# Byte rows for the first expansion, and its key gathers split in two, in a graph network kernel on one Trainium2 core

## The reference

```
edge network: h = relu([x_src, x_dst] @ W1.T + b1); v = h @ W2.T + b2, once for (src, dst), once for (dst, src)
              each v gives a Householder reflection; messages to src and to dst, scaled by 1/sqrt(deg) of both ends
              x = layernorm(x + relu(x - sum of messages))
two convolutions: h = tanh(segment_sum((h @ W)[src] * norm, dst) + b)
              x = layernorm(x + h)
```

## Time and profile before

| | |
|---|---|
| median of 3 runs | 7013.33 us |
| profiled execution, its time from first to last instruction (its span) | 7361.5 us |
| VectorE busy | 6335.9 us, 86% |
| ScalarE busy | 4842.1 us, 66% |
| TensorE matmul busy | 4369.6 us, 59% |
| GpSimd busy | 2840.7 us, 39% |
| first expansion | 1404 to 2343 us |
| key stage | 2345 to 2394 us |
| edge network | 2394 to 4700 us |

### The profile page before, as it was taken

One profiled execution on the slowest core, in us unless ns is written; L12 is line 12 of the kernel. 1 busy time (PEld: TensorE's weight loads), 2 busy tenths in 40 slices (PEclk: granted clock), 3 DMA queues, 4 the chain that ended last, 5 costly groups with the idle time before them and its releaser, 6 DMA issues.

```text
span 7361.5 us, 242681 instructions
## 1 busy us (share of the span) xinstructions
PE 4369.6 (59%) x83922; PEld 3504.3 (48%) x83922; DVE 6335.9 (86%) x9628; ACT 4842.1 (66%) x13310; POOL 2840.7 (39%) x2217
## 2 busy tenths in 40 slices
PE   1442000376665888888888888766566655566554
PEld 0342000266664555555555555555456544565443
DVE  4679997344445899999999999999999999999999
ACT  1665104122222899999999999899666677566776
POOL 5222304566764222222222222278500388200686
PEclk6666555688887898999889998887765699666898
DMA  4100000488876333333333333244499644799444
GB/s 63 8 8 8 4 0 26 148 297 298 299 288 218 120 117 118 116 118 116 116 116 116 117 117 117 88 121 120 105 294 291 211 120 120 200 293 295 127 121 95
DMA packets 510685, 1043.90 MB, mean 142 GB/s; under 512 B 125636, under 2 KB 316452, under 8 KB 497540
## 3 DMA queue, kind: packets, MB, share of 16 engines
q1 hardware_dynamic: 376804, 761.05, 30.1%
q0 software_dynamic: 113920, 281.72, 15.9%
q10 hardware_dynamic: 19872, 0.11, 0.2%
HBM read 756.44 MB, written 286.18 MB: 142 GB/s over the span
## 4 chain that ended last, share of the span: by engine, by line
DVE 28%; issue 27%; PE 12%; ACT 10%; POOL 10%; DVEq 5%; ACTq 3%; another core or an unknown queue 2%; DMA 1%; SPq 0%; POOLq 0%
PE ps L1118 7%; POOL got L638 4%; POOL sw_inb L638 4%; DVE xs_ring L1864 4%; PE ps L1259 3%; DVE wide_hotb L1987 3%; DVE keys L1476 3%; DVEq L1758 3%; ACT apartb L959 2%; DVE lane_hot L1754 2%; ACT step_lo L738 2%; DVE prods L1832 2%; ACTq L1006 2%; DVE keys L1475 2%
## 5 line engine op out<-in xcount | busy, mean ns | idle before, releaser
L638 POOL DMA_INDIRECT xs_ring<-xd_rows,src_idx x488 | 595.3, 1220 | 1803.8 <-DVE xs_ring L1864 1663.8
L1987 DVE TENSOR_SCALAR wide_hotb<-sw_inb,slot_id 128x2048 bf16<-128x2048 bf16 x976 | 923.2, 1014 | 57.5 <-PE ps L1259 57.3
L1754 DVE TENSOR_TENSOR wide_hotb<-dst_key,iota_b 128x1792 bf16<-128x1792 bf16 x879 | 949.0, 1080 | 8.5 <-ACT val_out L1017 4.4
L1259 PE MATMUL ps<-wide_tabb,wide_hotb 128*128 128x48 bf16 x15616 | 640.1, 207 | 360.9 <-DVE wide_hotb L1987 232.3
L638 POOL DMA_INDIRECT got<-val_rows,dst_idx x296 | 396.7, 1340 | 1177.3 <-DMA val_rows<-val_out 1085.9
L1118 PE MATMUL ps<-row_tab,dst_hot 128*128 128x64 bf16 x15744 | 656.0, 203 | 295.7 <-issue 244.9
L1259 PEld LDWEIGHTS ps<-wide_tabb,wide_hotb 128*128 128x128 bf16 x15616 | 592.0, 112 | 409.2 <-ACT val_out L1017 315.2
L1148 PEld LDWEIGHTS ps<-wide_tab,wide_hot 128*128 128x128 bf16 x23424 | 617.8, 99 | 347.8 <-DVE wide_hot L1748 309.1
L1118 PEld LDWEIGHTS ps<-row_tab,dst_hot 128*128 128x128 bf16 x15744 | 577.1, 104 | 374.9 <-issue 340.0
L638 POOL DMA_INDIRECT src_key<-chunk_keys,src_idx x488 | 622.0, 1275 | 335.5 <-ACT xd_out L801 187.3
L1148 PE MATMUL ps<-wide_tab,wide_hot 128*128 128x32 bf16 x23424 | 642.4, 181 | 89.0 <-DVE wide_hot L1748 84.0
(11 more groups left out here) (416 smaller groups left out, 11818.9 us busy)
## 6 DMA issues: line engine op xcount, KB each, us to landing
dw_in<-dst_wide SPq DMA_DIRECT2D x96, 1312.0 KB
xd_rows<-xd_out SPq DMA_DIRECT2D x128, 984.0 KB
sw_in<-src_wide SPq DMA_DIRECT2D x244, 512.0 KB
sw_inb<-src_wide SPq DMA_DIRECT2D x244, 512.0 KB, 5.1
val_rows<-val_out SPq DMA_DIRECT2D x488, 192.0 KB, 4.1
sw_inb<-src_byte SPq DMA_DIRECT2D x244, 256.0 KB, 4.4
msg_rows<-msg_out SPq DMA_DIRECT2D x244, 200.0 KB, 2.8
dw_in<-dst_byte SPq DMA_DIRECT2D x32, 656.0 KB
```

Of the source, the lines that this page charges most:

```text
L638: return pool.indirect_dma_start(out=into, out_offset=None, in_=table, in_offset=bass.IndirectOffsetOnAxis(index, 0))
L1259: last = mm(ps_val[s * 2 + h][:, t, :], wide_hot2[s][:, half, e:e + P], wide_tab2[s][:, h, half * 3 * D:(half + 1) * 3 * D], start=half == ...
L1754: return v.tensor_tensor(to.rearrange("p t (j k) -> p t j k", k=2), rel.unsqueeze(2).to_broadcast(shape), iota_b[:, 0:w].rearrange("p (j k ...
L1987: last = v.tensor_scalar(wide_hot2[q % 2][:, half, :], sw_in2[q][:, :], slot_id[:, half:half + 1], None, ALU.is_equal)
```

## The change

All rows of the first expansion are loaded as bytes. POOL gathers only `NA` = 288 steps of keys beside it (five steps in every two rows). The key stage works on these 288 x 8 = 2304 keys, in a form with fewer operations, and only 18 tiles are transposed and stored, the byte copy from the same transposes. The other 200 steps are gathered in the first 100 turns of the edge network, two steps in each, behind the turn's two row gathers, into the part of `dst_part` that is not used yet. In pass `MID` = 30 of the edge network's loop (counted from 0, so the 31st; it stands outside the hardware loop now) they are worked on in four rounds, one ahead of each turn. After the pass ACT and PE wait until all of it is done.

```diff
+    NA = 288
+    MID = 30
+    RATE = 2
+    TURNS = 4
+    ROUND = TURNS * P // CH
+    ROUNDS = ceil_div(NST - NA, ROUND)
+    PIECE = 256 // CH
...
-        dw_in = [sb(f"dw_in{k}", [P, WID], U8 if k == 3 else BF16, of=pc) for k in range(4)]
+        dw_in = [sb(f"dw_in{k}", [P, WID], U8, of=pc) for k in range(4)]
...
-                rows = dst_byte_v if k == 3 else dst_wide_v
+                rows = dst_byte_v
...
             sp.wait_ge(wide_stored, 32)
+            sp.wait_ge(rel_ready, 2)
...
+            def store_turned(r):
+                at = tiles_of(r)
+                sp.wait_ge(turn_copied, r + 3)
+                sp.dma_start(turn_v[:, at, :], turned_b[:, 0:at.stop - at.start, :]).then_inc(wide_stored, 16)
+                sp.dma_start(turn8_v[:, at, :], turned_b8[:, 0:at.stop - at.start, :]).then_inc(wide_stored, 16)
...
-            for s in range(NST):
-                if s % 4 == 0:
-                    pool.wait_ge(unit_copied, 3 * (2 + s // 4))
+            for s in range(NA):
+                if s % 5 == 0:
+                    pool.wait_ge(unit_copied, 3 * (2 + s // 5 * 2))
...
+                for s in range(NA + RATE * g, min(NA + RATE * g + RATE, NST)):
+                    gather(raw_b[:, (s - NA) * CH:(s - NA + 1) * CH], chunk_keys, src_idx[:, s:s + 1]).then_inc(keys_got, 16)
...
+            def copy_turned(r):
+                n = tiles_of(r).stop - tiles_of(r).start
+                act.wait_ge(rel_turned, r + 2)
+                if r > 0:
+                    act.wait_ge(wide_stored, 32 + 32 * r)
+                act.activation(turned_b[:, 0:n, :], ps_turn_b[:, 0:n, :], ACT.Copy)
+                act.activation(turned_b8[:, 0:n, :], ps_turn_b[:, 0:n, :], ACT.Copy).then_inc(turn_copied, 1)
...
+            for q in range(4):
+                turn(MID, q)
+                copy_turned(q)
+            act.wait_ge(rel_ready, ROUNDS + 4)
...
+            def turn_keys(r):
+                at = tiles_of(r)
+                pe.wait_ge(rel_ready, r + 4)
+                pe.wait_ge(xt_copied, MID * 4 + r + 2)
+                for c in range(at.start, at.stop):
+                    last = nc.tensor.transpose(ps_turn_b[:, c - at.start, :], src_rel[:, c * P:(c + 1) * P], ident_b[:, :])
+                last.then_inc(rel_turned, 1)
...
             step(v.tensor_scalar(half_i[:, :], half_i[:, :], 2 * P - 1, None, ALU.bitwise_and))
-            v.tensor_copy(src_low[:, 0:n], half_i[:, :]).then_inc(rel_ready, 1)
-            dve.wait_ge(rel_ready, 2)
-            step(v.tensor_tensor(missing[:, :], src_rel[:, 0:n], src_low[:, 0:n], ALU.not_equal))
-            step(v.tensor_scalar(missing[:, :], missing[:, :], 4.0 * P, None, ALU.mult))
-            step(v.tensor_tensor(dst_rel[:, 0:n], dst_rel[:, 0:n], missing[:, :], ALU.add))
+            step(v.tensor_tensor(missing[:, :], src_rel[:, 0:n], half_i[:, :], ALU.not_equal))
+            step(v.scalar_tensor_tensor(dst_rel[:, 0:n], missing[:, :], 4.0 * P, dst_rel[:, 0:n], ALU.mult, ALU.add))
...
+            def late_keys(r):
+                if r == 0:
+                    dve.wait_ge(keys_got, 16 * NST)
+                end = min(NA + (r + 1) * ROUND, NST)
+                for a in range(NA + r * ROUND, end, PIECE):
+                    b = min(a + PIECE, end)
+                    m, at, k = (b - a) * CH, slice(a * CH, b * CH), slice((a - NA) * CH, (b - NA) * CH)
+                    whole, half, gone, low_dst = raw_b_i[:, k], half_b[:, 0:m], missing_b[:, 0:m], dst_rel_b[:, 0:m]
+                    step(v.tensor_copy(whole, raw_b[:, k]))
+                    step(v.tensor_scalar(half, whole, 8, None, ALU.arith_shift_right))
+                    step(v.tensor_tensor(src_rel[:, at].rearrange("p (s c) -> p s c", c=CH), half.rearrange("p (s c) -> p s c", c=CH),
+                                         wide_base[:, a:b].unsqueeze(2).to_broadcast([P, b - a, CH]), ALU.subtract))
+                    v.tensor_scalar(whole, whole, 2 * P - 1, None, ALU.bitwise_and)
+                    step(v.tensor_scalar(half, half, 2 * P - 1, None, ALU.bitwise_and))
+                    step(v.tensor_tensor(gone, src_rel[:, at], half, ALU.not_equal))
+                    step(v.scalar_tensor_tensor(low_dst, gone, 4.0 * P, whole, ALU.mult, ALU.add))
+                    step(v.tensor_scalar(dst_part[:, at, 1], low_dst, float(P), None, ALU.is_ge))
+                    step(v.scalar_tensor_tensor(dst_part[:, at, 0], dst_part[:, at, 1], -float(P), low_dst, ALU.mult, ALU.add))
+                dve.sem_inc(rel_ready, 1)
+
+            def late_upper(r):
+                at = slice((NA + r * ROUND) * CH, min(NA + (r + 1) * ROUND, NST) * CH)
+                dve.wait_ge(rel_turned, r + 2)
+                step(v.tensor_scalar(src_upper[:, at], src_rel[:, at], float(P), None, ALU.is_ge))
+                step(v.scalar_tensor_tensor(src_rel[:, at], src_upper[:, at], -float(P), src_rel[:, at], ALU.mult, ALU.add))
+
+            with dve.Fori(1, MID) as i:
+                four_turns(i)
+            four_turns(MID)
+            late_upper(ROUNDS - 1)
+            dve.sem_inc(rel_ready, 1)
```

More of the change, by code:

```diff
@@ L52, in gnn_kernel @@
     G = NST // 2
+    assert NA % (P // CH) == 0 and ROUNDS == 4 and RATE * (4 * MID - 4) >= NST - NA and 8 * MID + 8 <= NA - 8
     assert NST % 4 == 0
@@ L136, in gnn_kernel @@
         place = sb("place", [P, WID], of=po)
+        before = sb("before", [P, P], of=po)
+        first = sb("first", [P, P], of=po)
+        iota_f = sb("iota_f", [P, P], of=po)
         follow = sb("follow", [P, P], of=po)
@@ L682, in _ @@
             pool.wait_ge(wide_stored, 32)
+            pool.wait_ge(rel_ready, 2)
             for g in range(G):
@@ L815, in _ @@
             act.wait_ge(rel_turned, 1)
[L816 to L822, removed]
+            for to in (turned, turned_8):
+                for b in range(0, NA * CH // P, 8):
+                    end = min(b + 8, NA * CH // P)
+                    last = act.activation(to[:, b:end, :], ps_turn[:, b:end, :], ACT.Copy)
+                last.then_inc(turn_copied, 1)
             act.wait_ge(wide_stored, 32)
-            act.wait_ge(rel_ready, 4)
+            act.wait_ge(rel_ready, 3)
             def tables(i, q):
@@ L934, in _ @@
                 turn(0, q)
-            with act.Fori(1, LAST) as i:
+            def copy_turned(r):
[5 more added lines that the diff above has]
+                act.activation(turned_b8[:, 0:n, :], ps_turn_b[:, 0:n, :], ACT.Copy).then_inc(turn_copied, 1)
+            with act.Fori(1, MID) as i:
+                for q in range(4):
+                    turn(i, q)
+            for q in range(4):
+                turn(MID, q)
+                copy_turned(q)
+            act.wait_ge(rel_ready, ROUNDS + 4)
+            with act.Fori(MID + 1, LAST) as i:
                 for q in range(4):
@@ L1126, in _ @@
                     expand_row(i, k)
-            pe.wait_ge(rel_ready, 2)
-            for c in range(LW * CH // P):
+            pe.wait_ge(rel_ready, 1)
+            for c in range(NA * CH // P):
                 last = nc.tensor.transpose(ps_turn[:, c, :], src_rel[:, c * P:(c + 1) * P], ident_b[:, :])
-            last.then_inc(rel_turned, 1)
-            for c in range(LW * CH // P):
-                last = nc.tensor.transpose(ps_turn8[:, c, :], src_low[:, c * P:(c + 1) * P], ident_b[:, :])
             last.then_inc(rel_turned, 1)
@@ L1206, in _ @@
                 turn(0, q)
-            with pe.Fori(1, LAST) as i:
+            def turn_keys(r):
[5 more added lines that the diff above has]
+                last.then_inc(rel_turned, 1)
+            with pe.Fori(1, MID) as i:
+                for q in range(4):
+                    turn(i, q)
+            for q in range(4):
+                turn(MID, q)
+                turn_keys(q)
+            pe.wait_ge(turn_copied, ROUNDS + 2)
+            with pe.Fori(MID + 1, LAST) as i:
                 for q in range(4):
@@ L1889, in _, with four_turns @@
             begun = done[0]
-            with dve.Fori(1, LAST) as i:
-                done[0], base[0] = 0, i * (LINKS * 4) + (begun - LINKS * 4)
+            extra = [0]
+            def four_turns(i):
+                done[0], base[0] = 0, i * (LINKS * 4) + (begun - LINKS * 4 + extra[0])
                 for q in range(4):
+                    if isinstance(i, int):
+                        late_keys(q)
+                        if q > 0:
+                            late_upper(q - 1)
                     turn(i, q)
-                assert done[0] == LINKS * 4, done[0]
@@ L1896, in _ @@
+            extra[0] = done[0] - LINKS * 4
+            dve.sem_inc(rel_ready, 1)
+            with dve.Fori(MID + 1, LAST) as i:
+                four_turns(i)
+            base[0], done[0] = 0, begun + (LAST - 1) * LINKS * 4 + extra[0]
             for q in range(4):
```

65 lines of the change are left out of this document (39 added, 26 removed).

## The result

The changed kernel takes 6907.88 us in the median of 4 runs (6905.14 to 6910.77), the kernel before 7013.13: a ratio of 0.9841, 95% interval 0.9819 to 0.9863, 105 us faster. The forecast was 6867, 146 faster.

What follows compares the result with a forecast made beforehand. DMA was taken to pace the first expansion, DVE the edge network. Expansion -171, key stage -14 and edge network +32 gave -153 us, scaled to -146: 7013 to 6867 us, 8-in-10 range 6745 to 6998.

Steps and rivals of the forecast that it cites:

- Part 1, the row: First expansion, all rows as bytes: a row falls from 7.34 to 6.0 us, 171 us saved over 128 rows.
- rival A: First expansion: PE's gaps shrink and DVE's floor sets the row, 4.75 to 5.2 us; 6733 us in all; chance 0.12.
- loop through PE: Expansion: copy, choose, hot and PE take 5.05 + P for two rows, P being PE's time on a row; 4.9 a row.
- sign of being right: Expected if the forecast holds: expansion of 740 to 800 us, DMA under 0.8 at about 280 GB/s.
- Part 1, POOL: First expansion: 2.5 gathers a row cost POOL at most 6.05 us, with 12 rows left to cover lateness.
- 0.953: Median 7013 over profiled span 7361.5; scales the summed change from -153 to -146 us, as the trace doesn't place the 348.
- Part 2, the key stage: Key stage: DVE's chain falls from 36.3 to 21.9 us, 14.4 saved; the other chain, 19.7, stays hidden.
- Part 3, the edge network: Edge network: moved gathers hidden, DVE's late work 25 us, the stall after pass 31 7 us; +32 in all.
- Rival D: Edge network: each of 200 gathers holds one DVE operation for 1.22 us, +244; 7100 us in all; chance 0.03.
- Rival B: First expansion: PE's 245 us of issue gaps stay, a row is 7.0 us; 6994 us in all; chance 0.16.
- Rival C: First expansion: the byte hot sits on each row's path, +132 us; 7156 us in all, slower; chance 0.07.

Runs made afterwards that it cites:

- late_wait: Changed kernel with ACT's wait for the late keys one pass of the edge network later: 7214.92 us, ratio 0.9814, where the kernel before took 7348.5.
- bytes_alone: Kernel before with all 128 rows as bytes and nothing else, all 488 key gathers still beside the expansion: 7137.35 us, ratio 1.0159.
- na240_b: Changed kernel with 240 key gathers beside the expansion instead of 288, the other 248 in the edge network, three a turn: 6856.43 us, ratio 0.9771.
- split_hot: Changed kernel with each byte hot cut into two instructions: 6864.26 us, ratio 0.977 to the kernel before.
- bf16_rows: Changed kernel with three of four rows loaded as bf16 again, the moved gathers kept: 6950.35 us, ratio 0.9891.
- after_again: Changed kernel, unchanged, run again as reference in the third group: 6913.67 us, ratio 0.9848.
- split_late: Changed kernel with the byte hot in two instructions and ACT's wait for the late keys one pass later: 6857.81 us, ratio 0.9765.
- na240: Changed kernel with 240 gathers beside the expansion, 248 in the edge network, in the second group: 7265.43 us, ratio 0.9879, where the kernel before took 7348.5.
- split_na240: Changed kernel with the byte hot in two instructions and 240 gathers beside the expansion: 7235.07 us, ratio 0.9852, where the kernel before took 7348.5.
- all_three: Changed kernel with two-instruction byte hot, 240 gathers beside the expansion and ACT's wait one pass later: 7229.24 us, ratio 0.9833, kernel before 7348.5.

## Why the prediction was right, and which terms were not

**The sign and the range** held: 6908 in 6745 to 6998, and the measured 105 us are 0.72 of the 146 forecast. That it came so near is in part luck, because errors cancel. In the executions that set the median the row before was 1.8 us shorter than the one costed and the row after 1.4 shorter than forecast, and a wait for keys that the sum doesn't have stands on both sides, 105 and 88 us.

**Part 1, the row.** I took 6.0 us a row, "the nearest thing that the trace shows to a row not held by DMA". It is 4.60 in the changed kernel. That is rival A's floor (4.75): DVE's hot and choose are 83.5% of the chain, and my loop through PE (5.05 + P)/2 gives 4.4 with a P of 3.8 (484 us of PE in 128 rows, at a granted clock of 1.00). What I counted against A, "P would have to be under 5 us", rested on PE's busy time at clocks of 0.80 to 0.94, in a profile whose gaps the ordinary executions don't have. The saving of 171 us was 122: the row came out shorter than forecast, but so was the row before, 5.55 us and not 7.34. In the condition that I had read, the row was right. late_wait has the changed kernel's expansion, and its profile, taken where the kernel before needs 7348.5 us, shows

```profile
1380.00:2130.00 750.00, 583.73 (x15744) 532.29 (x15743) 577.76 (x508) 274.77 (x636) 531.95 (x288) 0.93 0.75 283
```

That is 5.9 us a row, 188 us less than the 938 of the first profile, with all 288 gathers done in it. The mechanism of part 1 and its sign of being right (740 to 800 us, DMA under 0.8 at about 280 GB/s) are those of this condition, not of the runs that were measured.

**Part 1, POOL.** This is the step that failed. The prediction gave POOL 6.05 us a row for 2.5 gathers and set it against a row of 6.0 alone, so that the sum has no wait for keys. Its prices were about right, but one gather is held by each hot, so their number in a row falls with the row. In a row of the floor, 4.75 us, there is room for one held gather (3.39 + 0.30) and 0.7 others (1.27 + 0.30): 214 in 128 rows, with 74 left over, some 90 us at the 1.25 us that one takes alone. Measured: 222, 66 and 88. A gather beside byte hots takes 2.61 us from start to start, 6.5 for 2.5 of them. bytes_alone and na240_b show that the wait goes by the number of gathers: 200 more cost 255 us, 48 fewer save 60. split_hot shows that it goes by the length of the hot too.

**What the profile hid.** The kernel before also had this wait, 103 us, and nothing of it in the rows I read. So part 2's and 3's move of 200 gathers, which I counted as what "lets all rows be bytes", was itself the larger gain: bf16_rows, with the move alone, is 73 us under the kernel before, the bytes alone 114 over it, and both 105 under. The 348 us between span and median were the warning. I scaled them away as 0.953. Of the 343 between the spans of the two profiles 209 lay in the counting stage and 228 in the expansion, less the wait for keys, 105 in the second profile and 7 in the first; the rest, some 5, lay in the edge network.

**Part 2, the key stage:** -14.4 forecast, -14 measured: DVE's chain takes 22.7 us for the 21.9 forecast. The byte store did not come out on the path: SP's loads start at 1895.66 us, 0.1 behind the end of `dst_part`, whose semaphore they wait for.

**Part 3, the edge network:** +32 forecast, +46 measured. Pass 31 and the stall behind it cost 37 (five turns of 85.2 us against 48.4), of which the stall is 6.9 (forecast 7) and DVE's late work the rest, 30 for the 25 forecast. An operation of 256 elements takes 0.29 and 0.42 us where I had 0.24 and 0.41, as the timeline of that pass shows:

```profile
3114.45 0.29 DVE L1971 CAST dst_part<-dst_part 128x256 int32<-128x256 f32 x1
...
3116.10 0.42 DVE L1977 TENSOR_TENSOR missing_b<-src_rel,half_b 128x256 bf16<-128x256 bf16 x1
```

The other 10 are turns of 9.67 instead of 9.63 us, also those without gathers (130 to 240). after_again, bf16_rows and late_wait have them too, while split_hot, split_late and na240_b don't; they are not the gathers' and stay open.

**Rival D, the lock as the page "SBUF — State Buffer" of the Trainium skill has it (section "Who interferes with whom"),** did not come: DVE's wide_hot takes 751 ns beside twice the gathers (744 before, and 744 in after_again with the same gathers), and no DVE operation of the changed kernel between 1920 and 2900 us took over 0.15 us more than its usual time, where a gather's length is 0.94 or more. That page says that whoever issues first blocks the other. The runs agree in that POOL stands for the rest of a hot, and differ in the order: gathers that start up to 0.41 us before a hot are held by it all the same, and a hot is longer by 0.2 us at most, where a gather started 0.5 us ahead. **Rival B** did not come either, not even where PE has gaps of "issue": they are 135 us in late_wait's expansion and 118 in na240's, not 245, and a row is 5.9 and 5.7 us, not 7.0. **Rival C** had the right engine, DVE, on the path of each row, but what it replaced was longer.

## What to carry to other kernels

When the span of a profile is 5% over the median of the runs, find the stage that holds the difference before any stage is costed; here the disturbed one hid a wait of 103 us and showed gaps of 245 us that most runs don't have. When an edit makes a stage faster, set every engine's work beside it against the shorter stage at its best, not at the forecast: POOL's gathers had room in rows of 7.3 us, a little less than enough in rows of 5.5, and far from enough in 4.6. And an edit that lengthens one engine's instructions can slow another engine that never waits for it on a semaphore.

Of the versions tried, na240_b (0.9771) and split_late (0.9765) beat the kernel before by 164 and 163 us and the changed kernel by 57 and 56; the two can't be told apart from each other or, across groups, from split_hot (0.977), and split_late does without a third gather in a turn. Both edits of the hot and of the number of gathers together (split_na240, all_three) were run only where TensorE has its gaps.

## What the runs showed of the hardware that I had not expected

- Plain row transfers with the loads broadcast to 128 partitions ran at 389 GB/s and a DMA share of 0.99 for 712 us; in the condition of the first profile the same transfers stood at 295 GB/s and 0.81.
- Beside DVE's compare of 5248 bytes (2.94 us) a gather's issue on GpSimd takes up to 3.0 to 3.6 us instead of 0.94, also when it starts up to 0.41 us first, and ends 0.12 or 0.81 us behind the compare. DVE loses 0.2 us where a gather starts 0.5 us ahead. With the compare in two pieces (1.60 and 1.55 us) a gather takes about 1.9 to 2.1, in three it gets through between them in the first 49 rows of the profile and is then mostly held over all of them, 3.7 to 3.9.
- The same kernel takes 7013 to 7023 us in some groups of runs and 7348 in another, on another chip. In the longer condition TensorE stands in gaps of 0.5 us in the mean (up to 1.3, and 2.6 in the first profile) that no semaphore explains, in stages with hardly any DMA traffic too (the counting stage ends at 587 to 626 us instead of 417, with a DMA share of 0.09 in the first profile), and key gathers in the edge network then cost 0.4 us a turn for two and 1.3 for three, against 0.1 for three otherwise. The number of instruction fetches is the same in both conditions. What causes the gaps was not tried.
